# Narrow last matmuls, halved output and y steps, and a moved projection store in a GRU kernel

## The chip, the cores and the metric

The kernel runs on one core of a Trainium2 chip (trn2). The metric is the device time of one execution in microseconds; lower is better. One core has five engines that run side by side, each with its own queue in program order: PE (TensorE, matmuls), DVE (VectorE), ACT (ScalarE), POOL (GpSimd) and SP (SyncE), which here only issues DMAs. They meet through semaphores.

## The reference, cut to what matters

```python
# x: (2, 2048, 512) fp32, cond: (2, 512)
h = silu(cond @ W1.T + b1); gate = sigmoid(h @ W2.T + b2)[:, None, :]
# a Haar analysis and synthesis with every coefficient times gate: gives gate * v
x = x + (v + a)                       # v = x, so this is y = x * (2 + gate)
# GRU over 2048 time steps, batch 2, width 512, h0 = 0
vz, vr, vh = cond @ C_z + b_z, cond @ C_r + b_r, cond @ C + b
xz, xr, xh = y @ W_z, y @ W_r, y @ W  # one row for each time step
def step(h, xs):
    z = sigmoid(xz_t + h @ U_z + vz)
    r = sigmoid(xr_t + h @ U_r + vr)
    hh = tanh(xh_t + r * h @ U + vh)
    return (1.0 - z) * h + z * hh
out = y + (h of every step)
```

The steps of the GRU depend on each other, so they run one after the other: 2048 of them.

## The kernel before, in words

Width 512 lies on 128 partitions in K = 4 chunks; with batch 2 a state is 128 x 8 numbers. Each U is split into two fp16 parts, and so are h and r*h, so that sums of fp16 products have nearly fp32 accuracy. The new h is never put together for PE: it is given as four fp16 pieces (kept part high and low, new part high and low, `h_part`), r*h as two (`rh_part`).

One **step** has three products on PE, r, z and h, each of 32 matmuls of 128x128 weights (4 output chunks m, 4 input chunks k, 2 weight parts; `tile_product`, L247, the matmul is at L252). The moving operand has 8 columns (h: 4), repeated to fill WIDE = 32 columns of the output's slot in PSUM. Only the last 8 (or 4) columns of a slot and the two behind it, which ACT seeds with the input's projection (L335, L337), are read: `total` (L487) on DVE adds them up. r and h are in two halves in two banks, `staggered` (L257), so that they can start on half of their input and their first total can start early; z (L285 to L288) is one product with one total. ACT takes a tanh of each total (L351), and of z's it makes `z_keep` and `z_mul` (L368, L369), which L522 and the rest of DVE's tail need. DVE makes `rh_part` (L496, L500, L505) and at the end `h_part` (L522 to L541) and `h_cur` (L553). The first half of `h_part` releases the next step's r product. ACT also copies `h_cur` into the ring `hist` (L363).

A **block** is TB = 64 time steps: TURN = 4 steps written out (u = 0 to 3), and then GM = 12 bodies of BODY = 5 steps; NB = 32 blocks. Work beside the recurrence is put behind single steps:

- Each body makes one of the 12 tiles of the next block's input projection: in its steps u = 0 to 3 PE does one matmul (L224) of `w_stage` with `y_next` behind the h product. The tile's weights come by DMA into the one buffer `w_stage` (SP, L166), which is loaded anew for each body after the projection before it is done. In u = 0 PE waits for that load (L295) ahead of its matmul. After step u = 3 DVE stores the tile into the ring `xp` (`store_projection`, L558), after a wait for PE.
- In the turn: after step 0 PE transposes the block after next from `x_tok` into `ps_x`, and DVE makes the sum of hist and y_cur for the output, `oT` (`make_out`, L564). After step 1 PE transposes oT into `ps_o` (`put_out`), and ACT copies `y_next` to `y_cur` (L377). After step 2 ACT copies `ps_o` to `o_tok` (`put_out`, L384), and DVE makes the new `y_next` (`make_y`, L455).

**SP's queue** in a block, in this order: wait for x_tr, load the next x_tok (L131); wait for o_ev (ACT's copy to o_tok), store the output (L135, two DMAs); then twelve times: wait for proj_mm, load w_stage (L166). The queue is in order, so what is behind a wait waits too.

Of the kernel before, what the change touches and what calls it, by code (L numbers as in the profile page):

```python
# [13 lines left out]
P = 128  # L14
# [5 lines left out]
def gru_kernel(nc, x, cond, W1, b1, W2, b2, W_z, U_z, C_z, b_z, W_r, U_r, C_r, b_r, W, U, C, b, out):  # L20
# [25 lines left out]
    with ExitStack() as ctx:  # L46
# [36 lines left out]
        hist = sb("hist", [P, 2 * TB, S])  # L83
# [88 lines left out]
        @block.gpsimd  # L172
        def _(pool):
            nc.gpsimd.memset(ident[:, :], 0.0).then_inc(s["ident_zero"], 1)
            pool.wait_ge(s["ident_zero"], 1)
            nc.gpsimd.affine_select(out=ident[:, :], in_=ident[:, :], compare_op=ALU.not_equal, fill=1.0,
                                    base=0, pattern=[[-1, P]], channel_multiplier=1).then_inc(s["ident_ok"], 1)

            nc.gpsimd.memset(h_cur[:, :], 0.0)
            nc.gpsimd.memset(hist[:, TB:2 * TB, :], 0.0)  # L180
            nc.gpsimd.memset(y_cur[:, :, :], 0.0)
            nc.gpsimd.memset(h_part[:, 0:HC], 0.0).then_inc(s["hs0"], 1)
            nc.gpsimd.memset(h_part[:, HC:K], 0.0).then_inc(s["hs1"], 1)
            nc.gpsimd.memset(xp[:, :, TB:2 * TB, :], 0.0).then_inc(s["h0_ready"], 1)
            pool.wait_ge(s["umax_ok"], G)
            nc.gpsimd.partition_all_reduce(u_all[:, :], u_max[:, :], P, RMAX).then_inc(s["uall_ok"], 1)

        @block.tensor
        def _(pe):
# [40 lines left out]
            pe.wait_ge(s["y_ok"], 1)  # L230
# [16 lines left out]
            def tile_product(bank, m, g, gm, k, parts, first):  # L247

                n = (ADDENDS[g] - 1) * B
                moving = parts[:, k, :, :].rearrange("p a b -> p (a b)").unsqueeze(1).broadcast_to([P, WIDE // n, n])  # L250
                for part in range(PARTS):
                    last = nc.tensor.matmul(bank[:, SLOT * m:SLOT * m + WIDE].rearrange("p (r n) -> p r n", n=n),  # L252
                                            u_part[:, g, part, k, gm * P:(gm + 1) * P], moving,
                                            start=first and part == 0, stop=False, skip_group_check=True)
                return last

            def staggered(banks, g, parts, src, name, t1):  # L257


                def product(mh, m, kh):  # L260
                    for k in range(kh * HC, (kh + 1) * HC):
                        last = tile_product(banks[mh], m, g, mh * HC + m, k, parts, k == 0 and m == 0)
                    return last
# [15 lines left out]
            def steps(t0, count, proj=None, turn=None):  # L279
                for u in range(count):  # L280
# [4 lines left out]
                    for m in range(K):  # L285
                        for k in range(K):
                            last = tile_product(ps_z, m, Z, m, k, h_part, k == 0 and m == 0)
# [16 lines left out]
                    if turn is not None and u == 1:  # L304
                        put_out(turn[1])

            def put_out(nb):
                pe.wait_ge(s["o_sum"], nb)
# [12 lines left out]
        def _(act):  # L321
# [31 lines left out]
            def steps(t0, count, ring, turn=None):  # L353

                for u in range(count):
# [7 lines left out]
                    A(hist[:, prv, :], h_cur[:, :], ACT.Copy)  # L363
# [27 lines left out]
            A(hist[:, (T - 1) % (2 * TB), :], h_cur[:, :], ACT.Copy).then_inc(s["copied"], 1)  # L391
# [3 lines left out]
        def _(dve):  # L395
# [62 lines left out]
            make_y(1)  # L458
# [31 lines left out]
            def step(t1):  # L490
# [26 lines left out]
                total(ps_z, Z, K, "z_sum")  # L517
                dve.wait_ge(s["h0_mm"], t1)
# [36 lines left out]
            def store_projection(count, i, ring):  # L555

                dve.wait_ge(s["proj_mm"], count)
# [4 lines left out]
            def make_out(ring):  # L562

                V.scalar_tensor_tensor(oT[:, :, :], hist[:, bass.ds(ring, TB), :].rearrange("p t c -> p c t"), 1.0 / H_SCALE,  # L564
                                       y_cur[:, :, :], ALU.mult, ALU.add).then_inc(s["o_sum"], 1)

            def steps(t0, count, proj=None, turn=None):


                for u in range(count):  # L570
                    step(dve.snap(t0 + (u + 1)))
                    if proj is not None and u == K - 1:
                        store_projection(*proj)
                    if turn is not None and u == 0:

                        make_out(turn[0])
                    if turn is not None and u == 2:
                        dve.wait_ge(s["y_copied"], turn[1])
                        make_y(turn[2])

            with dve.Fori(0, NB) as n:
                other = dve.snap(((n + 1) % 2) * TB)
                steps(dve.snap(n * TB), TURN, turn=(other, dve.snap(n + 1), dve.snap(n + 2)))
                with dve.Fori(0, GM) as i:

                    steps(dve.snap(n * TB + i * BODY + TURN), BODY, proj=(dve.snap(n * GM + i + 2), i, other))
            dve.wait_ge(s["copied"], 1)
            make_out((NB - 1) % 2 * TB)
# [26 lines left out]
```

## Time and profile before

| | |
|---|---|
| median of the runs | 6800.1 us (3 runs, 6799.94 to 6800.25) |
| the profiled execution | 6811.76 us, of which the span from first to last instruction is 6809.9 |
| mean granted TensorE clock | 0.996 of full speed |
| busy | PE 5998.4 us (88%), weight loads 5642.2 (83%), DVE 4955.6 (73%), ACT 3331.6 (49%) |
| DMA | q1: 80304 packets, 129.81 MB, 5.5% of 16 engines |

How to read it: an engine's busy time is the sum over its instructions, with overlaps counted once. PE and DVE start an instruction before the one ahead has ended, so a duration is longer than the distance to the next start. On the timeline, instructions of one kind that follow each other are merged into one row: start, time from the first start to the last end, and the number behind x. The part in brackets tells how long the engine was idle before the row and what released it. The profiled execution's own time, not the median, is what the rows below add up to.

### The profile page before, as it was taken

The numbers are of one execution on the slowest core, as the hardware profiler recorded it, in microseconds if no ns is written. First come the engines' busy times: TensorE is split into PE (matmuls) and PEld (weight loads), VectorE is DVE, ScalarE is ACT, GpSimd is POOL, SyncE is SP. The second block draws the span as 40 slices with busy tenths as digits, with TensorE's granted clock in tenths as the row PEclk, the third lists the DMA queues.
The fourth block names the chain that finished last, engine by engine and source line by source line (L and its number), as shares of the span: only waits on it lengthen the run. The fifth ranks groups of instructions, "written<-read, shape, count | busy, mean of one in ns | idle before, by whom it ended". The sixth has DMA issues, their size and how long they took to land.

```text
span 6809.9 us, 488240 instructions
## 1 busy us (share of the span) xinstructions
PE 5998.4 (88%) x200232; PEld 5642.2 (83%) x200232; DVE 4955.6 (73%) x43503; ACT 3331.6 (49%) x22603; POOL 3.5 (0%) x13
## 2 busy tenths in 40 slices
PE   7888888888888888888888888888888888888888
PEld 7888888888888888888888888888888888888888
DVE  5777777777777777777777777777777777777777
ACT  3444444444444444444444444444444444444444
POOL 0000000000000000000000000000000000000000
PEclk8999999999999999999999999999999999999999
DMA  2000000000000000000000000000000000000000
GB/s 84 17 18 15 18 17 18 17 17 17 18 17 18 15 18 17 18 18 15 18 17 18 17 18 15 18 17 18 17 17 17 18 17 18 15 18 18 17 18 15
DMA packets 80315, 129.97 MB, mean 19 GB/s; under 512 B 12336, under 2 KB 18480, under 8 KB 80304
## 3 DMA queue, kind: packets, MB, share of 16 engines
q1 hardware_dynamic: 80304, 129.81, 5.5%
q8 instruction: 8, 0.13, 0.0%
q14 instruction: 3, 0.02, 0.0%
HBM read 20.46 MB, written 8.65 MB: 4 GB/s over the span
## 4 chain that ended last, share of the span: by engine, by line
PE 71%; DVE 26%; issue 3%; SPq 0%; DMA 0%; ACT 0%; ACTq 0%; DVEq 0%
PE pair_r L252 30%; PE ps_z L252 24%; PE pair_h L252 17%; DVE pair_h L487 8%; DVE h_part L522 5%; DVE h_part L541 4%; DVE h_part L527 2%; DVE keep L523 2%; DVE zn L536 2%; DVE h_part L532 2%; PE ps_z L212 0%; DMA u_raw<-in_L_cond_U 0%; PE ps_o L212 0%; DVE u_max L424 0%; PE ps_x L224 0%
## 5 line engine op out<-in xcount | busy, mean ns | idle before, releaser
L252 PEld LDWEIGHTS pair_r<-h_part,u_part 128*128 128x128 f16 x65536 | 1845.1, 96 | 1119.9 <-DVE h_part L541 1115.8
L252 PE MATMUL pair_r<-h_part,u_part 128*128 128x32 f16 x65536 | 2048.7, 177 | 771.1 <-DVE h_part L541 758.6
L252 PE MATMUL pair_h<-rh_part,u_part 128*128 128x32 f16 x65536 | 2016.6, 177 | 12.5 <-DVE rh_part L505 12.5
L252 PE MATMUL ps_z<-h_part,u_part 128*128 128x32 f16 x65536 | 1961.5, 176 | 0.0
L252 PEld LDWEIGHTS pair_h<-rh_part,u_part 128*128 128x128 f16 x65536 | 1842.8, 96 | 17.3 <-DVE rh_part L505 15.7
L252 PEld LDWEIGHTS ps_z<-h_part,u_part 128*128 128x128 f16 x65536 | 1795.3, 95 | 0.0
L487 DVE TENSOR_REDUCE pair_r<-pair_r 128x4 f32<-128x20 f32 x4096 | 759.4, 186 | 818.1 <-PE pair_r L252 615.1
L351 ACT ACTIVATE pair_r<-pair_r 128x4 f32<-128x4 f32 x4096 | 644.8, 158 | 1445.1 <-DVE pair_r L487 1182.4
L487 DVE TENSOR_REDUCE pair_h<-pair_h 128x4 f32<-128x12 f32 x4096 | 717.7, 175 | 665.7 <-PE pair_h L252 665.7
L351 ACT ACTIVATE th_z<-ps_z 128x8 f32<-128x8 f32 x2048 | 364.1, 178 | 1046.0 <-DVE ps_z L487 1046.0
L337 ACT ACTIVATE pair_h<-xp 128x8 f32 (+1 forms) x2049 | 369.9, 181 | 807.8 <-DVE zn L536 807.8
L505 DVE TENSOR_TENSOR rh_part<-rh,rh_part 128x4 f16<-128x4 f32 x4096 | 662.2, 162 | 141.1
L541 DVE TENSOR_TENSOR h_part<-zn,h_part 128x4 f16<-128x4 f32 x4096 | 669.6, 163 | 70.5
L224 PE MATMUL ps_p<-y_next,w_stage 128*128 128x128 f32 x3072 | 718.1, 316 | 0.0
L351 ACT ACTIVATE pair_h<-pair_h 128x4 f32<-128x4 f32 x4096 | 647.2, 158 | 102.2
L496 DVE SCALAR_TENSOR_TENSOR rh_part<-pair_r,h_cur 128x4 f16<-128x4 f32 x4096 | 649.6, 159 | 6.0
L532 DVE TENSOR_TENSOR h_part<-z_mul,pair_h 128x4 f16<-128x4 f32 x4096 | 625.6, 153 | 0.0
L500 DVE SCALAR_TENSOR_TENSOR rh<-pair_r,h_cur 128x4 f32<-128x4 f32 x4096 | 621.8, 152 | 0.0
L536 DVE TENSOR_TENSOR zn<-z_mul,pair_h 128x4 f32<-128x4 f32 x4096 | 619.8, 151 | 0.0
L224 PEld LDWEIGHTS ps_p<-y_next,w_stage 128*128 128x128 f32 x3072 | 458.2, 188 | 0.0
L363 ACT ACTIVATE hist<-h_cur 128x8 f32 x2048 | 428.2, 209 | 4.4
L487 DVE TENSOR_REDUCE ps_z<-ps_z 128x8 f32<-128x40 f32 x2048 | 421.8, 206 | 0.0
(70 smaller groups left out, 3275.9 us busy)
## 6 DMA issues: line engine op xcount, KB each, us to landing
w_stage<-w_in SPq DMA_DIRECT2D x384, 256.0 KB, 2.3
x_tok<-in_x SPq DMA_DIRECT2D x68, 128.0 KB, 2.6
out_dram<-o_tok SPq DMA_DIRECT2D x66, 128.0 KB, 2.3
mlp_w<-in_L_cond_W SPq DMA_DIRECT2D x2, 1024.0 KB, 6.9
u_raw<-in_L_cond_U_r SPq DMA_DIRECT2D x1, 1024.0 KB, 5.6
u_raw<-in_L_cond_U_z SPq DMA_DIRECT2D x1, 1024.0 KB, 7.6
u_raw<-in_L_cond_U SPq DMA_DIRECT2D x1, 1024.0 KB, 10.3
w_in<-in_L_cond_W_r SPq DMA_DIRECT2D x4, 256.0 KB, 9.8
```

The costliest lines, as they stand in the source:

```text
L224: return nc.tensor.matmul(bank[:, col:col + P], weight[:, k, :], y_next[:, k * B:(k + 1) * B, :].rearrange("p b t -> p (b t)"), start=(k = ...
L252: last = nc.tensor.matmul(bank[:, SLOT * m:SLOT * m + WIDE].rearrange("p (r n) -> p r n", n=n), u_part[:, g, part, k, gm * P:(gm + 1) * P] ...
L337: return A(to[:, :, :, WIDE:SLOT], src.rearrange("p (h m) b -> p h m b", h=2), ACT.Copy)
L351: A(to, bank[:, SUM:SUM + n], ACT.Tanh, scale=scale_reg[g]).then_inc(s[done], 1)
L363: A(hist[:, prv, :], h_cur[:, :], ACT.Copy)
L487: return V.tensor_reduce(bank[:, SUM:SUM + m * B].rearrange("p (m b) -> p m b", b=B), cols(bank, g, 0, m).rearrange("p m a b -> p m b a"), ...
L496: V.scalar_tensor_tensor(rh_part[:, kc[hf], 0, :], kb(ps_r[hf][:, TANH:TANH + HS]), 1.0, kb(h_cur[:, half[hf]]), ALU.add, ALU.mult)
L500: V.scalar_tensor_tensor(rh[:, half[hf]], ps_r[hf][:, TANH:TANH + HS], 1.0, h_cur[:, half[hf]], ALU.add, ALU.mult).then_inc(s[f"rh32_{hf}" ...
L505: V.tensor_tensor(rh_part[:, kc[hf], 1, :], kb(rh[:, half[hf]]), rh_part[:, kc[hf], 0, :], ALU.subtract).then_inc(s[f"rh{hf}"], 1)
L532: V.tensor_tensor(h_part[:, kc[hf], NEW, :], kb(z_mul[:, half[hf]]), kb(ps_h[hf][:, TANH:TANH + HS]), ALU.mult)
L536: V.tensor_tensor(zn[:, half[hf]], z_mul[:, half[hf]], ps_h[hf][:, TANH:TANH + HS], ALU.mult).then_inc(s[f"zn{hf}"], 1)
L541: V.tensor_tensor(h_part[:, kc[hf], NEW + 1, :], kb(zn[:, half[hf]]), h_part[:, kc[hf], NEW, :], ALU.subtract).then_inc(s[f"hs{hf}"], 1)
```

## The change

- `tile_product` takes `closing`: the last matmul (second weight part, k = 3) of the last output chunk of each total writes only the columns that are read, 8 of 32 for r and z, 4 of 32 for h. There are five in a step: r's two halves, z, h's two halves.
- `hist` has its time axis last, so that `make_out` reads it contiguously and ACT writes it with a stride.
- `make_out`, the copy to `y_cur` and `make_y` are in two halves of 4 of the 8 chunks each. make_out's are after turn steps 0 and 1, the copy's after 1 and 2, make_y's after 2 and 3. PE's `put_out` (transposes of oT) moves from after step 1 to after step 2, ACT's `put_out` (o_tok) from after step 2 to after step 3. The waits count halves.
- `store_projection` moves from the end of a body's step u = 3 into its step u = 4, right behind z's total, without the wait for proj_mm.
- SP's queue is as before.

```diff
-        hist = sb("hist", [P, 2 * TB, S])
+        hist = sb("hist", [P, S, 2 * TB])
...
-            def tile_product(bank, m, g, gm, k, parts, first):
+            def tile_product(bank, m, g, gm, k, parts, first, closing=False):
 
                 n = (ADDENDS[g] - 1) * B
-                moving = parts[:, k, :, :].rearrange("p a b -> p (a b)").unsqueeze(1).broadcast_to([P, WIDE // n, n])
+                own = parts[:, k, :, :].rearrange("p a b -> p (a b)")
+                slot = bank[:, SLOT * m:SLOT * m + WIDE]
                 for part in range(PARTS):
-                    last = nc.tensor.matmul(bank[:, SLOT * m:SLOT * m + WIDE].rearrange("p (r n) -> p r n", n=n),
-                                            u_part[:, g, part, k, gm * P:(gm + 1) * P], moving,
+                    weight = u_part[:, g, part, k, gm * P:(gm + 1) * P]
+                    if closing and part == PARTS - 1:
+
+                        return nc.tensor.matmul(slot[:, WIDE - n:WIDE], weight, own, start=False, stop=False, skip_group_check=True)
+                    last = nc.tensor.matmul(slot.rearrange("p (r n) -> p r n", n=n), weight,
+                                            own.unsqueeze(1).broadcast_to([P, WIDE // n, n]),
                                             start=first and part == 0, stop=False, skip_group_check=True)
                 return last
...
-                        last = tile_product(banks[mh], m, g, mh * HC + m, k, parts, k == 0 and m == 0)
+                        last = tile_product(banks[mh], m, g, mh * HC + m, k, parts, k == 0 and m == 0,
+                                            m == HC - 1 and k == K - 1)
...
-                            last = tile_product(ps_z, m, Z, m, k, h_part, k == 0 and m == 0)
+                            last = tile_product(ps_z, m, Z, m, k, h_part, k == 0 and m == 0, m == K - 1 and k == K - 1)
...
-                    if turn is not None and u == 1:
+                    if turn is not None and u == 2:
                         put_out(turn[1])
 
             def put_out(nb):
-                pe.wait_ge(s["o_sum"], nb)
+                pe.wait_ge(s["o_sum"], nb * 2 if isinstance(nb, int) else pe.snap(nb * 2))
...
-                y_count = pe.snap(n + 2)
+                y_count = pe.snap(n * 2 + 4)
...
-                    A(hist[:, prv, :], h_cur[:, :], ACT.Copy)
+                    A(hist[:, :, bass.ds(prv, 1)], h_cur[:, :].unsqueeze(2), ACT.Copy)
...
-                    if turn is not None and u == 1:
-                        act.wait_ge(s["o_sum"], turn)
-                        A(y_cur[:, :, :], y_next[:, :, :], ACT.Copy).then_inc(s["y_copied"], 1)
-                    if turn is not None and u == 2:
+                    if turn is not None and u in (1, 2):
+                        act.wait_ge(s["o_sum"], act.snap(turn * 2 + (u - 2)))
+                        A(y_cur[:, half[u - 1], :], y_next[:, half[u - 1], :], ACT.Copy).then_inc(s["y_copied"], 1)
+                    if turn is not None and u == 3:
                         put_out(turn)
...
-            def make_y(nb):
-
+            def make_y(part, nb, n=None):
                 dve.wait_ge(s["x_tr"], nb)
-                V.tensor_tensor(y_next[:, :, :], ps_x[:, :].rearrange("p (c t) -> p c t", t=TB),
-                                gate2[:, :].unsqueeze(2).broadcast_to([P, S, TB]), ALU.mult).then_inc(s["y_ok"], 1)
+                if n is not None:
+                    dve.wait_ge(s["y_copied"], dve.snap(n * 2 + (part + 1)))
+                V.tensor_tensor(y_next[:, half[part], :], ps_x[:, :].rearrange("p (c t) -> p c t", t=TB)[:, half[part], :],
+                                gate2[:, half[part]].unsqueeze(2).broadcast_to([P, HS, TB]), ALU.mult).then_inc(s["y_ok"], 1)
...
                 total(ps_z, Z, K, "z_sum")
+                if proj is not None:
+                    store_projection(*proj)
                 dve.wait_ge(s["h0_mm"], t1)
...
-            def store_projection(count, i, ring):
-
-                dve.wait_ge(s["proj_mm"], count)
+            def store_projection(i, ring):
+
                 V.tensor_tensor(xp[:, i, bass.ds(ring, TB), :].rearrange("p t b -> p b t"),
...
-            def make_out(ring):
-
-                V.scalar_tensor_tensor(oT[:, :, :], hist[:, bass.ds(ring, TB), :].rearrange("p t c -> p c t"), 1.0 / H_SCALE,
-                                       y_cur[:, :, :], ALU.mult, ALU.add).then_inc(s["o_sum"], 1)
+            def make_out(part, ring):
+
+                V.scalar_tensor_tensor(oT[:, half[part], :], hist[:, half[part], bass.ds(ring, TB)], 1.0 / H_SCALE,
+                                       y_cur[:, half[part], :], ALU.mult, ALU.add).then_inc(s["o_sum"], 1)
...
-                    step(dve.snap(t0 + (u + 1)))
-                    if proj is not None and u == K - 1:
-                        store_projection(*proj)
-                    if turn is not None and u == 0:
-
-                        make_out(turn[0])
-                    if turn is not None and u == 2:
-                        dve.wait_ge(s["y_copied"], turn[1])
-                        make_y(turn[2])
+                    step(dve.snap(t0 + (u + 1)), proj if u == K else None)
+                    if turn is not None and u < 2:
+                        make_out(u, turn[0])
+                    if turn is not None and u >= 2:
+                        make_y(u - 2, turn[2], turn[1])
```

## Rows read from the trace of the kernel before

**Rows 1.** Page, the chain that ended last: share of the span by engine.
```profile
PE 71%; DVE 26%; issue 3%; SPq 0%; DMA 0%; ACT 0%; ACTq 0%; DVEq 0%
```

**Rows 2.** Timeline, a plain step: start us, us, engine, line, op, out<-in, count [idle<-releaser].
```profile
3011.66 1.00 PE L252 MATMUL pair_r<-h_part,u_part 128*128 128x32 f16 x32 [0.31 <-DVE h_part L541]
...
3012.39 0.49 DVE L487 TENSOR_REDUCE pair_r<-pair_r 128x4 f32<-128x20 f32 x2 [0.38 <-PE pair_r L252]
...
3012.51 0.96 PE L252 MATMUL ps_z<-h_part,u_part 128*128 128x32 f16 x32
...
3013.41 0.16 DVE L505 TENSOR_TENSOR rh_part<-rh,rh_part 128x4 f16<-128x4 f32 x1
3013.50 0.21 DVE L487 TENSOR_REDUCE ps_z<-ps_z 128x8 f32<-128x40 f32 x1
3013.75 0.18 ACT L351 ACTIVATE th_z<-ps_z 128x8 f32<-128x8 f32 x1 [0.52 <-DVE ps_z L487]
...
3014.03 0.18 DVE L487 TENSOR_REDUCE pair_h<-pair_h 128x4 f32<-128x12 f32 x1 [0.32 <-PE pair_h L252]
...
3014.12 0.30 PEld L224 LDWEIGHTS ps_p<-y_next,w_stage 128*128 128x128 f32 x2
...
3014.20 0.17 DVE L522 TENSOR_TENSOR h_part<-z_keep,h_cur 128x8 f16<-128x8 f32 x1
...
3014.92 1.00 PE L252 MATMUL pair_r<-h_part,u_part 128*128 128x32 f16 x32 [0.30 <-DVE h_part L541]
```

**Rows 3.** Timeline, the next step, which has the projection's store; last row: next r.
```profile
3015.51 0.29 DVE L558 TENSOR_TENSOR xp<-ps_p,v_bias 128x128 f32 x1 [0.24 <-issue]
3015.72 0.42 DVE L487 TENSOR_REDUCE pair_r<-pair_r 128x4 f32<-128x20 f32 x2
...
3017.04 0.18 ACT L351 ACTIVATE th_z<-ps_z 128x8 f32<-128x8 f32 x1 [0.55 <-DVE ps_z L487]
...
3017.54 0.17 DVE L522 TENSOR_TENSOR h_part<-z_keep,h_cur 128x8 f16<-128x8 f32 x1
...
3018.26 0.52 PE L252 MATMUL pair_r<-h_part,u_part 128*128 128x32 f16 x13 [0.64 <-DVE h_part L541]
```

**Rows 4.** Timeline, turn step 1, with make_out; first and last row: its r and the next.
```profile
3021.54 1.00 PE L252 MATMUL pair_r<-h_part,u_part 128*128 128x32 f16 x32
...
3021.85 1.09 DVE L564 SCALAR_TENSOR_TENSOR oT<-hist,y_cur 128x512 f32<-128x512 f32 x1
...
3025.36 0.29 PE L252 MATMUL pair_r<-h_part,u_part 128*128 128x32 f16 x5
```

**Rows 5.** Timeline, turn step 3: r, make_y, o_tok, SP's queue, and the next r.
```profile
3028.62 1.00 PE L252 MATMUL pair_r<-h_part,u_part 128*128 128x32 f16 x32 [0.62 <-DVE h_part L541]
...
3028.89 0.68 DVE L455 TENSOR_TENSOR y_next<-ps_x,gate 128x512 f32<-128x512 f32 x1
3028.94 0.59 ACT L384 ACTIVATE o_tok<-ps_o 128x512 f32<-128x512 f32 x1
...
3029.75 1.27 SPq L135 DMA_DIRECT2D out_dram<-o_tok  x2
...
3031.39 0.53 SPq L166 DMA_DIRECT2D w_stage<-w_in  x1
...
3032.00 0.27 PE L252 MATMUL pair_r<-h_part,u_part 128*128 128x32 f16 x4 [0.62 <-DVE h_part L541]
```

**Rows 6.** Line 558, 3015.0 to 3015.9: ns min/median/max, first to last start, of register code.
```profile
L558 DVEq FUSED_REGOPS  x2: 52/112/173, 3015.2 to 3015.4; - x2
```

**Rows 7.** DMA issues from 3025 to 3040: count, KB each, median us to landing.
```profile
w_stage<-w_in SPq DMA_DIRECT2D x1, 256.0 KB, 2.3
```

**Rows 8.** Timeline of PE, the first step of all and the start of the second.
```profile
74.90 1.03 PE L252 MATMUL pair_r<-h_part,u_part 128*128 128x32 f16 x32 [3.88 <-issue]
...
78.36 0.81 PE L252 MATMUL pair_r<-h_part,u_part 128*128 128x32 f16 x23
```

**Rows 9.** Windows: us, busy of PE, PEld, DVE, ACT, POOL, granted clock, DMA share, GB/s.
```profile
75.00:79.00 4.00, 4.00 (x123) 3.91 (x123) 2.79 (x22) 1.65 (x11) 0.00 (x0) 0.51 0.01 4
```

More of the change, by code:

```diff
@@ L179, in _ @@
             nc.gpsimd.memset(h_cur[:, :], 0.0)
-            nc.gpsimd.memset(hist[:, TB:2 * TB, :], 0.0)
+            nc.gpsimd.memset(hist[:, :, TB:2 * TB], 0.0)
             nc.gpsimd.memset(y_cur[:, :, :], 0.0)
@@ L229, in _ @@
             pe.wait_ge(s["w_ok"], G)
-            pe.wait_ge(s["y_ok"], 1)
+            pe.wait_ge(s["y_ok"], 2)
             pe.wait_ge(s["gate_ok"], 1)
@@ L390, in _ @@
             act.wait_ge(s["h_ok"], T)
-            A(hist[:, (T - 1) % (2 * TB), :], h_cur[:, :], ACT.Copy).then_inc(s["copied"], 1)
+            A(hist[:, :, (T - 1) % (2 * TB)], h_cur[:, :], ACT.Copy).then_inc(s["copied"], 1)
             put_out(NB + 1)
@@ L450, in _ @@
             dve.wait_ge(s["gate_ok"], 1)
-            def make_y(nb):
+            def make_y(part, nb, n=None):
                 dve.wait_ge(s["x_tr"], nb)
-                V.tensor_tensor(y_next[:, :, :], ps_x[:, :].rearrange("p (c t) -> p c t", t=TB),
-                                gate2[:, :].unsqueeze(2).broadcast_to([P, S, TB]), ALU.mult).then_inc(s["y_ok"], 1)
-            make_y(1)
+                if n is not None:
+                    dve.wait_ge(s["y_copied"], dve.snap(n * 2 + (part + 1)))
+                V.tensor_tensor(y_next[:, half[part], :], ps_x[:, :].rearrange("p (c t) -> p c t", t=TB)[:, half[part], :],
+                                gate2[:, half[part]].unsqueeze(2).broadcast_to([P, HS, TB]), ALU.mult).then_inc(s["y_ok"], 1)
+            for part in range(2):
+                make_y(part, 1)
             for g in range(G):
@@ L488, in total, with step @@
                                        cols(bank, g, 0, m).rearrange("p m a b -> p m b a"), AX_X, ALU.add).then_inc(s[done], 1)
-            def step(t1):
+            def step(t1, proj):
                 kc = (slice(0, HC), slice(HC, K))
@@ L560, in store_projection @@
                                 v_bias[:, i, :].unsqueeze(2).broadcast_to([P, B, TB]), ALU.add)
-            def make_out(ring):
-                V.scalar_tensor_tensor(oT[:, :, :], hist[:, bass.ds(ring, TB), :].rearrange("p t c -> p c t"), 1.0 / H_SCALE,
-                                       y_cur[:, :, :], ALU.mult, ALU.add).then_inc(s["o_sum"], 1)
+            def make_out(part, ring):
+                V.scalar_tensor_tensor(oT[:, half[part], :], hist[:, half[part], bass.ds(ring, TB)], 1.0 / H_SCALE,
+                                       y_cur[:, half[part], :], ALU.mult, ALU.add).then_inc(s["o_sum"], 1)
             def steps(t0, count, proj=None, turn=None):
                 for u in range(count):
-                    step(dve.snap(t0 + (u + 1)))
-                    if proj is not None and u == K - 1:
-                        store_projection(*proj)
-                    if turn is not None and u == 0:
-                        make_out(turn[0])
-                    if turn is not None and u == 2:
-                        dve.wait_ge(s["y_copied"], turn[1])
-                        make_y(turn[2])
+                    step(dve.snap(t0 + (u + 1)), proj if u == K else None)
[3 more added lines that the diff above has]
+                        make_y(u - 2, turn[2], turn[1])
             with dve.Fori(0, NB) as n:
                 other = dve.snap(((n + 1) % 2) * TB)
-                steps(dve.snap(n * TB), TURN, turn=(other, dve.snap(n + 1), dve.snap(n + 2)))
+                steps(dve.snap(n * TB), TURN, turn=(other, n, dve.snap(n + 2)))
                 with dve.Fori(0, GM) as i:
-                    steps(dve.snap(n * TB + i * BODY + TURN), BODY, proj=(dve.snap(n * GM + i + 2), i, other))
+                    steps(dve.snap(n * TB + i * BODY + TURN), BODY, proj=(i, other))
             dve.wait_ge(s["copied"], 1)
-            make_out((NB - 1) % 2 * TB)
+            for part in range(2):
+                make_out(part, (NB - 1) % 2 * TB)
 _INS = ["x", "cond_1024", "L0_cond_W1", "L0_cond_b1", "L0_cond_W2", "L0_cond_b2",
```

## The prediction, made before the changed kernel was run

> **What bounds the kernel now.** I read the chain of waits first: PE holds 71% of the chain that ended last and DVE 26%, DMA nothing [rows 1]. So one recurrent step, 2048 times in a row, sets the time. Then I read a plain step on the timeline [rows 2]. From one start of the r product (3011.66) to the next (3014.92) it takes 3.26 us. PE streams r, z and h, then totals on DVE, tanhs on ACT and the tail on DVE release the next r. The wait that ends last in it is z's: z's product ends at 3012.51+0.96 = 3013.47, its total starts at 3013.50, th_z at 3013.75, and L522, which needs ACT's z_keep, at 3014.20, 0.72 us ahead of the next r. DVE is free for z's total at about the same time, since L505 starts at 3013.41 and a DVE instruction can start 0.08 us before the one ahead of it ends (L558 ends at 3015.80, the total behind it starts at 3015.72 [rows 3]).
>
> Third, I compare steps by their r starts. The step with the projection's store takes 3018.26-3014.92 = 3.34 [rows 2, 3]. The four turn steps take 3.28, 3.82, 3.26 and 3.38 [rows 3 to 5]. The others are plain: one block is 4 turn steps and 12 bodies of 5 steps, 32 times. Last, I read SP's queue: nearly idle, but it feeds w_stage [rows 5].
>
> **Narrow closing matmul, L252.** Five products a step get a last matmul of 8 (h: 4) columns instead of 32. PE's stream is not shortened by it: r's 32 matmuls start within 3012.51-3011.66 = 0.85 us, at most 27 ns each [rows 2], and no row shows them closer. Only the end of each product can come earlier. The bounds: nothing, and 24/32 of 27 ns, 20 ns. I take 10 ns, the middle, which is also one column per cycle at the full clock of 2.4 GHz. Then r's totals, L505 and z's total come 10 ns earlier and take th_z, z_keep and L522 along. 2048 x 0.010 = 20.5 us gained, between 0 and 41.
>
> The Trainium skill (TensorE: Matmul & The Clock Gate, "Single matmul latency") gives a latency of (398+N)/2.4 ns; by it 24 columns are 10 ns. No row here has a narrower fp16 matmul to compare.
>
> **Output and y in halves, L564, L455.** L564 starts at 3021.85, 0.31 into turn step 1, and takes 1.09; total r0 should start 3012.39-3011.66 = 0.73 in [rows 2, 4]. The step is longer by 0.56. y's 0.68 us make step 3 longer by 0.12 [rows 5]. A half has 256 elements. From 128 elements in 0.29 (L558) and 512 in 0.68 (L455), 256 take 0.42; at L564's strided pace they take 0.16+0.93/2 = 0.62. A half that starts at 0.31 frees DVE at 0.65 or at 0.85, against 0.73. The new hist layout makes the reads contiguous, so I take the first: hidden in all four steps, (0.56+0.12) x 32 = 21.8 us gained. By the other end two halves would cost 0.12 each, 8 us. ACT's halves of y_cur and its strided write of hist fall where ACT waits for totals. The new waits are met beforehand: ahead of each half of y DVE waits for a copy that ACT made one step earlier, and PE's transposes of oT, now after step 2, wait for halves made after steps 0 and 1. The 0.02 of turn step 0 has none of this in it and stays.
>
> The Trainium skill (SBUF — State Buffer, "Door 1: The DMA port swizzle") says that each access that crosses to a new 16-byte line pays a penalty. hist was read 32 bytes apart; 1.09 us against 0.68 for as many elements agrees, and by the rule the halves are at the fast end.
>
> **Projection's store behind z's total, L558.** The store step is 0.08 longer, but part of it isn't the store: from th_z to L522 it takes 3017.54-3017.04 = 0.50 against 0.45 in the plain step [rows 2, 3], all of it ACT's own work, so that stays. The store's share is that th_z comes 2.12 into the step instead of 2.09, 0.03 to 0.04 with the rounding. 384 x 0.035 = 13.4 us gained if the new place hides it. There DVE is free from z's total (1.83 into the step after the change) to h0's total (now 3014.03, 2.37 in; then some 2.35). The store's address code starts at 3015.2 and is two pieces, 52 and 173 ns, the store at 3015.51: 0.30 with gaps [rows 3, 6]. The store holds DVE for 0.29-0.08 = 0.21. 1.83+0.02+0.30+0.21 = 2.36: it just fits, and L522 behind it waits for ACT until 2.6.
>
> **The step that is moved with them: o_tok on ACT, and SP behind it.** put_out on ACT moves from after turn step 2 to after turn step 3. SP's queue is left as it is, and in order: wait for o_tok, store the output (L135, two DMAs), and only then load w_stage for body 0 (L166). Before, o_tok starts at 3028.94, the stores go from 3029.75, L166 at 3031.39 [rows 5], and its data land 2.3 later [rows 7], at 3033.7. A projection comes 3014.12-3011.66 = 2.46 into its step [rows 2], here 3032.00+2.46 = 3034.46: 0.8 us to spare. After the change the same row of events hangs on the r start of body step 0 as it hung on 3028.62: the data land 3031.39+2.3-3028.62 = 5.07 into that step, and the projection wants them at 2.46. PE waits, and behind it in its queue stands the next step's r product, for which DVE and ACT wait in turn. PE goes on at 5.07+0.03, the projection's weight loads take 0.30 [rows 2], so r starts at 5.40 instead of 3.25: 2.15 us lost per block, x 32 = 68.8 us.
>
> PE then stands idle for some 2.4 us in each block. Recurrent steps at half clock are seen only at the start: after 3.88 us of idle PE the clock is at 0.51, and the step from 74.90 to 78.36 takes 3.46 instead of turn step 0's 3.28 [rows 8, 9]. I count one such step per block, 0.17 x 32 = 5.5 us, with bounds of none and two.
>
> **Sum.** The profiled execution took 6811.8 us (span 6809.9), 11.7 above the median of the runs; the terms are counts of steps, so I put them against the median. 6800.1 - 20.5 - 21.8 - 13.4 + 68.8 + 5.5 = 6818.7, say 6818, with 6806 to 6830 for the clock's bounds and some ns in each term. About 0.2%, 13.6 us, is what a measurement of this kernel can tell from no change, so this is just slower.
>
> **Rivals.**
> - *No earlier ends.* What ends a product is the way through PE and the semaphore, not the columns. For it: r's last matmul ends 3011.66+1.00-3012.51 = 0.15 after z's first has started [rows 2], so most of a matmul's time isn't its columns. Then 20.5 us are missing: 6839. Chance 0.17.
> - *Store collides with h0's total.* The address code is longer in the new place. For it: the fit above has no spare. If it takes half as long again, 0.15, of which ACT's lateness hides 0.04, 384 x 0.11 = 42 us come on top: 6860. Chance 0.08.
> - *No stall, so faster.* The one mechanism is SP's: if w_stage has landed 2.46 into body step 0, the 68.8 and the 5.5 fall away: 6744. It needs L166 issued by 2.46-2.3 = 0.16 into that step, while o_tok starts only 0.32 into it. Each 0.1 us beyond costs 3.2 us, so faster by 0.2% needs a stall under 1.3 us. Rows 5 show nothing that lets SP pass the store. Chance 0.08.
> - *Terms a little better*: the clock stays up, the columns are worth up to 20 ns, or the stall is 0.2 us shorter: 6795 to 6812, no difference that can be measured. Chance 0.15.
>
> **How the numbers follow.** The forecast has 0.52; a third of its 6806 to 6830 lies within 0.2%. Slower: 0.35+0.17+0.08 = 0.60. Same: 0.17+0.13 = 0.30. Faster: 0.08+0.02 = 0.10. The range, 6795 to 6842, takes in the bounds of the columns and of the clock; it leaves out the faster case and the full collision.
>
> **What would show it.** Right: once a block PE idle for some 2.4 us ahead of L224, ended by the DMA of w_stage; plain steps of 3.25, turn steps of 3.27 and three of 3.25, a store step of 3.29 to 3.30; z's total 1.83 into a step; h0's total in the store step not behind 2.37; halves of 0.42. A mean granted clock under the 0.996 of before would show the clock's term. Wrong: plain steps still of 3.26 (columns), a store step above 3.34 (collision), no DMA among the releasers of L224 (no stall), many steps at half clock, each 0.17 us.

## The result and the profile after

| | before | after |
|---|---|---|
| median of the runs | 6800.5 us (6 runs) | 6839.7 us (6835.6 to 6845.6, 6 runs) |
| ratio to before | | 1.0058, 95% interval 1.0045 to 1.0071 |
| the profiled execution | 6811.8 us, span 6809.9 | 6840.6 us, span 6838.8 |
| mean granted TensorE clock | 0.996 | 0.957 |

The kernel became slower by 39.2 us, 0.58%. The kernel before runs some 10 us longer at some times than at others (medians of 6799.8 and of 6809.6 on the same chip), and its trace is of a long run, which is why the two spans lie only 28.9 us apart. Ratios below are to runs of before made together with the kernel named. The line numbers of the kernel after: matmuls L257, the narrow one L256, totals L495, tanhs L357, L522 is now L532, the store L558 is L567, make_out L573, make_y L462, o_tok L390.

The waits of the kernel after over its whole execution (engine, line, what it waited for: us in total, times, longest) show one wait that was not there before:

```profile
PE pair_r L257 <- DVE h_part L551: 723.7, 1840, 0.7
...
PE ps_p L224 <- DMA w_stage<-w_in: 83.7, 32, 3.8
```

PE waits 32 times, once a block, 2.6 us each, for the load of w_stage. The timeline of one body step 0 (rows of PE, ACT and SP; it answers to rows 5, which showed turn step 3 before):

```profile
3043.47 0.67 PE L257 MATMUL pair_r<-h_part,u_part 128*128 128x32 f16 x19 [0.63 <-DVE h_part L551]
3043.79 0.59 ACT L390 ACTIVATE o_tok<-ps_o 128x512 f32<-128x512 f32 x1
...
3044.60 1.27 SPq L135 DMA_DIRECT2D out_dram<-o_tok  x2
...
3045.92 0.16 PE L256 MATMUL pair_h<-rh_part,u_part 128*128 128x4 f16 x1
3046.24 0.53 SPq L166 DMA_DIRECT2D w_stage<-w_in  x1
3048.67 0.50 PEld L224 LDWEIGHTS ps_p<-y_next,w_stage 128*128 128x128 f32 x2 [2.67 <-issue]
3048.67 0.79 PE L224 MATMUL ps_p<-y_next,w_stage 128*128 128x128 f32 x2 [2.59 <-DMA w_stage<-w_in]
3049.05 0.82 PEld L257 LDWEIGHTS pair_r<-h_part,u_part 128*128 128x128 f16 x19
3049.26 0.71 PE L257 MATMUL pair_r<-h_part,u_part 128*128 128x32 f16 x19
```

It reads as forecast: o_tok 0.32 into the step, the stores at 1.13, L166 at 2.77, its data 2.31 later at 5.08, and the projection, wanted at 2.46, starts at 5.20. The next r starts 5.79 after this one, 0.59 behind the projection.

Here the granted clock went to half at 3048.63, just ahead of the projection. In the block shown next it did so only behind r's start (1782.28 on this timeline), and r comes 0.32 behind the projection, 5.53 into the step:

```profile
1776.31 0.68 PE L257 MATMUL pair_r<-h_part,u_part 128*128 128x32 f16 x19 [0.63 <-DVE h_part L551]
...
1781.52 0.48 PE L224 MATMUL ps_p<-y_next,w_stage 128*128 128x128 f32 x2 [2.60 <-DMA w_stage<-w_in]
1781.84 0.65 PE L257 MATMUL pair_r<-h_part,u_part 128*128 128x32 f16 x19
```

A plain step after, on the timeline (it answers to rows 2), and below it the halves and the store by line:

```profile
3072.22 0.67 PE L257 MATMUL pair_r<-h_part,u_part 128*128 128x32 f16 x19 [0.31 <-DVE h_part L551]
...
3073.86 0.17 PE L256 MATMUL ps_z<-h_part,u_part 128*128 128x8 f16 x1
...
3074.06 0.21 DVE L495 TENSOR_REDUCE ps_z<-ps_z 128x8 f32<-128x40 f32 x1
3074.30 0.18 ACT L357 ACTIVATE th_z<-ps_z 128x8 f32<-128x8 f32 x1 [0.51 <-DVE ps_z L495]
...
3075.47 0.67 PE L257 MATMUL pair_r<-h_part,u_part 128*128 128x32 f16 x19 [0.30 <-DVE h_part L551]
```

```profile
L256 PE MATMUL pair_r<-h_part,u_part 128*128 128x8 f16 x4096 | 680.5, 166 | 0.0
...
L567 DVE TENSOR_TENSOR xp<-ps_p,v_bias 128x128 f32 x384 | 112.1, 292 | 47.0
...
L573 DVE SCALAR_TENSOR_TENSOR oT<-hist,y_cur 128x256 f32<-128x256 f32 x66 | 27.7, 422 | 0.4 <-ACT hist L397 0.4
L462 DVE TENSOR_TENSOR y_next<-ps_x,gate 128x256 f32<-128x256 f32 x66 | 27.7, 420 | 0.2 <-PE ps_x L194 0.2
```

The step takes 3.25 us, the halves 0.42 each, as forecast, and the narrow matmul lasts 166 ns.

All traces together, from one r product's first matmul to the next one's (ns; turn and body steps are means over blocks 2 to 32, the plain and the store step medians, so that single falls of the clock don't enter there). The last column has the number and the sum of the stretches at half clock, 1.2 of 2.4 GHz, after the first 100 us; each such stretch is called a fall below. The last of them reaches to the end of the execution, when the steps are over; before has no other.

| kernel | turn steps 0, 1, 2, 3 | body 0, step 0 | step 1 | plain | store | half clock |
|---|---|---|---|---|---|---|
| before | 3285, 3825, 3258, 3382 | 3258 | 3258 | 3259 | 3340 | 1, 9 us |
| after | 3341, 3264, 3244, 3244 | 5757 | 3347 | 3245 | 3289 | 132, 543 us |
| o_tok back | 3324, 3265, 3244, 3394 | 3279 | 3263 | 3243 | 3288 | 108, 373 us |
| o_tok late only | 3282, 3825, 3256, 3378 | 5652 | 3334 | 3254 | 3331 | 32, 139 us |
| closing only | 3405, 3720, 3250, 3372 | 3317 | 3296 | 3245 | 3331 | 277, 997 us |
| after, no closing | 3274, 3255, 3253, 3254 | 5774 | 3368 | 3255 | 3299 | 32, 195 us |
| closing, 40 columns | 3277, 3821, 3247, 3371 | 3246 | 3250 | 3246 | 3338 | 1, 6 us |
| z only, 40 columns | 3284, 3831, 3266, 3386 | 3264 | 3267 | 3267 | 3333 | 1, 7 us |
| all but z, 40 columns | 3273, 3818, 3263, 3370 | 3259 | 3262 | 3262 | 3338 | 1, 8 us |
| store only | 3285, 3831, 3258, 3383 | 3257 | 3257 | 3257 | 3304 | 1, 6 us |
| halves, load first | 3275, 3256, 3258, 3259 | 3258 | 3257 | 3258 | 3341 | 1, 8 us |
| 24 columns | 3483, 3743, 3282, 3403 | 3353 | 3351 | 3352 | 3392 | 31, 6501 us |
| after, 40 columns | 3261, 3250, 3246, 3246 | 5679 | 3756 | 3246 | 3292 | 31, 156 us |
| after, load first, 40 columns | 3261, 3247, 3249, 3250 | 3249 | 3248 | 3250 | 3292 | 1, 7 us |

### The profile page after: what moved, and what is told of

Its sections match the earlier page's. It is cut to its first block, busy times and chain, and to the rows that moved or that the text cites. A ratio compares the mean times of both kernels' runs of the same rounds, so it can differ in the third digit from the quotient of the medians.

```text
span 6838.8 us, 488018 instructions
## 1 busy us (share of the span) xinstructions
PE 5991.9 (88%) x200232; PEld 5641.6 (82%) x200232; DVE 4947.4 (72%) x43569; ACT 3310.3 (48%) x22635; POOL 3.5 (0%) x13
## 4 chain that ended last, share of the span: by engine, by line
PE 64%; DVE 28%; issue 3%; ACT 3%; DMA 1%; SPq 1%; ACTq 0%; DVEq 0%
PE pair_r L257 28%; PE ps_z L257 19%; PE pair_h L257 13%; DVE pair_h L495 6%; DVE h_part L532 5%; DVE h_part L551 4%; DVE h_part L537 2%; DVE keep L533 2%; DVE rh_part L513 2%; DVE zn L546 2%; DVE h_part L542 2%; PE ps_p L224 1%; DMA w_stage<-w_in 1%; DVE pair_r L495 1%; ACT pair_r L343 1%
## 5 line engine op out<-in xcount | busy, mean ns | idle before, releaser
L257 PEld LDWEIGHTS pair_r<-h_part,u_part 128*128 128x128 f16 x61440 | 1805.0, 96 | 1080.1 <-DVE h_part L551 1072.6
L257 PE MATMUL pair_r<-h_part,u_part 128*128 128x32 f16 x61440 | 2004.7, 178 | 735.0 <-DVE h_part L551 723.7
L257 PE MATMUL pair_h<-rh_part,u_part 128*128 128x32 f16 x61440 | 1936.5, 177 | 0.0
L257 PE MATMUL ps_z<-h_part,u_part 128*128 128x32 f16 x63488 | 1918.2, 177 | 0.0
L257 PEld LDWEIGHTS pair_h<-rh_part,u_part 128*128 128x128 f16 x61440 | 1771.3, 96 | 0.0
L257 PEld LDWEIGHTS ps_z<-h_part,u_part 128*128 128x128 f16 x63488 | 1751.9, 96 | 0.0
L495 DVE TENSOR_REDUCE pair_r<-pair_r 128x4 f32<-128x20 f32 x4096 | 765.5, 187 | 1044.9 <-PE pair_r L256 804.7
L357 ACT ACTIVATE pair_r<-pair_r 128x4 f32<-128x4 f32 x4096 | 647.2, 158 | 1497.1 <-DVE pair_r L495 1224.1
L495 DVE TENSOR_REDUCE pair_h<-pair_h 128x4 f32<-128x12 f32 x4096 | 713.1, 174 | 514.3 <-PE pair_h L256 514.3
L357 ACT ACTIVATE th_z<-ps_z 128x8 f32<-128x8 f32 x2048 | 364.0, 178 | 1029.9 <-DVE ps_z L495 1029.9
L224 PE MATMUL ps_p<-y_next,w_stage 128*128 128x128 f32 x3072 | 760.7, 331 | 83.7 <-DMA w_stage<-w_in 83.7
L357 ACT ACTIVATE pair_h<-pair_h 128x4 f32<-128x4 f32 x4096 | 647.1, 158 | 128.8
L256 PE MATMUL pair_r<-h_part,u_part 128*128 128x8 f16 x4096 | 680.5, 166 | 0.0
L256 PE MATMUL pair_h<-rh_part,u_part 128*128 128x4 f16 x4096 | 672.3, 164 | 0.0
L542 DVE TENSOR_TENSOR h_part<-z_mul,pair_h 128x4 f16<-128x4 f32 x4096 | 621.8, 152 | 0.1
L224 PEld LDWEIGHTS ps_p<-y_next,w_stage 128*128 128x128 f32 x3072 | 486.7, 200 | 86.3 <-issue 86.3
## 6 DMA issues: line engine op xcount, KB each, us to landing
u_raw<-in_L_cond_U SPq DMA_DIRECT2D x1, 1024.0 KB, 11.1
```

The costliest lines, as they stand in the source:

```text
L224: return nc.tensor.matmul(bank[:, col:col + P], weight[:, k, :], y_next[:, k * B:(k + 1) * B, :].rearrange("p b t -> p (b t)"), start=(k = ...
L256: return nc.tensor.matmul(slot[:, WIDE - n:WIDE], weight, own, start=False, stop=False, skip_group_check=True)
L257: last = nc.tensor.matmul(slot.rearrange("p (r n) -> p r n", n=n), weight, own.unsqueeze(1).broadcast_to([P, WIDE // n, n]), start=first a ...
L357: A(to, bank[:, SUM:SUM + n], ACT.Tanh, scale=scale_reg[g]).then_inc(s[done], 1)
L495: return V.tensor_reduce(bank[:, SUM:SUM + m * B].rearrange("p (m b) -> p m b", b=B), cols(bank, g, 0, m).rearrange("p m a b -> p m b a"), ...
L542: V.tensor_tensor(h_part[:, kc[hf], NEW, :], kb(z_mul[:, half[hf]]), kb(ps_h[hf][:, TANH:TANH + HS]), ALU.mult)
```

## The experiments

The theory was this: the loss is the stall behind o_tok; the three edits proper each gain what the steps show; and a second loss is in the clock, since the trace of after falls to half clock 132 times where before it fell once, at its end. The stall explains at most one fall a block, so either the narrow matmuls cause the rest, or the falls have one cause and follow the stall in ways not seen. The first four kernels tell these apart.

**o_tok back.** The kernel after, with ACT's copy where it was:

```diff
-                    if turn is not None and u == 3:
+                    if turn is not None and u == 2:
                         put_out(turn)
```

> The changed kernel with one thing undone: ACT copies o_tok after turn step 2 again. Theory (the load of w_stage stands behind o_tok and the output's store in SP's queue): the stalled step of 5.9 us a block goes back to 3.25, 2.65 us x 32 = 85 us less than the changed kernel, about 6754; PE waits for no DMA ahead of L224; some falls of the clock stay, because the narrow closing matmuls stream fewer columns: mean clock about 0.98. Rival (the falls of the clock come only from PE's idle time in the stall): mean clock 0.996 again, as before the change, and 6744. Rival (the stall has another cause, such as the wait for y in halves): about 6840 still.

Measured: 6760.0 us, ratio 0.9942 (0.9926 to 0.9959), mean clock 0.970; no wait for w_stage is left. That is 79.7 less than after, against 85 expected. The difference is a new cost in turn step 3, 3394 ns instead of 3244, 4.8 us over 32 blocks. Its timeline, r to r:

```profile
3002.63 0.67 PE L257 MATMUL pair_r<-h_part,u_part 128*128 128x32 f16 x19
3002.95 0.40 ACT L383 ACTIVATE y_cur<-y_next 128x256 f32<-128x256 f32 x1
...
3003.25 0.58 ACT L390 ACTIVATE o_tok<-ps_o 128x512 f32<-128x512 f32 x1
3003.35 0.49 DVE L495 TENSOR_REDUCE pair_r<-pair_r 128x4 f32<-128x20 f32 x2
3003.73 0.30 ACT L357 ACTIVATE pair_r<-pair_r 128x4 f32<-128x4 f32 x2
...
3006.02 0.24 PE L257 MATMUL pair_r<-h_part,u_part 128*128 128x32 f16 x3 [0.62 <-DVE h_part L551]
```

The half of y_cur and o_tok now stand behind the same step on ACT, and r's tanh starts 0.38 after its total instead of 0.22 (3013.33 to 3013.55 in a plain step of the same trace). So the copy's new place had its use. The rival by which the falls come only from the stall is out: without a stall 107 remain, and the one at the end.

**o_tok late only.** The kernel before, with that one edit:

```diff
-                    if turn is not None and u == 2:
+                    if turn is not None and u == 3:
                         put_out(turn)
```

> The kernel before with this alone: ACT copies o_tok after turn step 3 instead of step 2. Theory: r of body step 1 starts 5.55 us after that of step 0 instead of 3.26, and the half clock after it costs 0.3 us more: 2.6 us x 32 = +84, about 6884. If the stall needs the halves or the moved transposes: 6800.

Measured: 6880.5 us, ratio 1.0119 (1.0102 to 1.0136), +80.7 us, near the 84 expected, with one fall at each stall. One moved line of ACT costs it all; halves, transposes and store are not needed for it. The waits of this kernel:

```profile
PE ps_p L224 <- DMA w_stage<-w_in: 82.7, 32, 3.2
```

**Closing only.** The kernel before with the changed `tile_product` and the two places that use it. Cut to the line that matters:

```diff
+                    if closing and part == PARTS - 1:
+
+                        return nc.tensor.matmul(slot[:, WIDE - n:WIDE], weight, own, start=False, stop=False, skip_group_check=True)
```

> The kernel before with the narrow closing matmuls alone. Theory: plain steps 3.244 instead of 3.258 us, 2048 x 0.014 = -29; the clock falls for one stretch some two or three times a block, +10: about 6782, clock about 0.98. Rival (falls come from the stall only): no fall after the first 100 us, 6772. Rival (columns bring nothing): 6800 and steps of 3.258.

Measured: 6810.9 us, ratio 1.0015 (1.0006 to 1.0025), +11.1 where -18 was expected. The plain step is as expected, 3245 against the 3255 of the kernels with full matmuls that ran together with it (o_tok late only; after, no closing): 10 ns. But the clock fell 277 times, not two or three times a block, and stood at half for 997 us. Windows of the granted clock around one of these stretches (us, busy of PE, PEld, DVE, ACT, POOL, granted clock, DMA share, GB/s):

```profile
3029.00:3032.40 3.40, 2.78 (x104) 2.65 (x101) 2.44 (x24) 1.63 (x12) 0.00 (x0) 1.00 0.56 154
3032.50:3035.90 3.40, 3.40 (x107) 3.14 (x104) 2.43 (x23) 1.63 (x12) 0.00 (x0) 0.50 0.00 0
3035.90:3039.30 3.40, 3.08 (x111) 2.89 (x108) 2.46 (x22) 1.56 (x11) 0.00 (x0) 1.00 0.00 0
```

With 10 ns x 2048 = 20 us gained and 11 lost on the whole, the falls cost 31 us, 0.11 us each. They come in 235 of the 384 bodies, and 224 of the 277 start in a body's step 0, behind the store step, the one step with no projection's matmul behind h. I had read the number of falls to expect off the kernel after, where that step is 3289 ns long; here the store is in its old place and it is 3331. Whether that difference is why there are more falls here, no run shows.

**After without closing.** All calls pass `closing` as False.

```diff
-                                            m == HC - 1 and k == K - 1)
+                                            False)
...
-                            last = tile_product(ps_z, m, Z, m, k, h_part, k == 0 and m == 0, m == K - 1 and k == K - 1)
+                            last = tile_product(ps_z, m, Z, m, k, h_part, k == 0 and m == 0, False)
```

> The changed kernel with full closing matmuls. Theory: plain steps 3.258, and the clock falls only once a block, behind the stall: 6840 + 29 - 10 = about 6858, clock about 0.975. Rival (falls have nothing to do with the columns): as many falls as in the changed kernel, about four a block, and 6869.

Measured: 6855.6 us, ratio 1.0079 (1.0062 to 1.0096), clock 0.982, and no fall but those at the stalls and the end. The narrow matmuls are what adds the 100 other falls. Taking them out costs 15.9 us over after, where 18 were expected (the intervals of the two ratios overlap a little): in the change as a whole they seem to gain more than their falls cost.

The second four ask whether it is the number of columns, and which of the five closing matmuls matter.

**Closing, 40 columns.** The closing-only kernel with one constant changed. The extra columns are copies that nothing reads, as the ones before.

```diff
-    WIDE = 32
+    WIDE = 40
```

> The kernel before with the narrow closing matmuls, and all other matmuls of the step 40 columns wide instead of 32. Theory (the clock falls because PE streams too few columns in a stretch): no fall after the first 100 us, plain steps stay 3.244, 6800 - 29 = 6771. Rival (it is the narrow matmul itself that upsets the clock, or the shorter step): about as many falls as with 32 columns, 277 of them, and 6811. Rival (40 columns no longer fit the pace of 25 ns): each step longer by up to 96 x 3 ns, over 7000.

Measured: 6791.3 us, ratio 0.9975 (0.9965 to 0.9984), -18.2 us; no fall between the start and the end, clock 0.996, plain step 3246. The narrow matmul is harmless once the others carry more columns, and 40 still fit the pace. The gain is smaller than the 29 I had written. That took 3258 and 3244 from the two first traces, which are not of runs made together; and not every step gains as much. A plain step gains 12 ns (3246 against 3257 or 3258 in before, store only and halves), but the store step only 2 (3338 against 3340), and the mean block of the trace is 209.63 us long against 210.23 before: 19 us in 32 blocks.

**Only z narrow**, and **all but z narrow**, both with 40 columns:

> As b2 but narrow only in z's last matmul. Theory (z's total is the last wait of the step and the h0 chain 11 ns behind it): plain steps 3.247, about 11 of the 14 ns, 6800 - 23 = 6777. Rival (r's and h's chain is the last): 3.258, 6800.

> As b2 but narrow in r's and h's last matmuls and not in z's. Theory: nothing gained, z's last matmul with 40 columns ends 3 ns later than with 32: plain steps 3.258 to 3.262, 6800 to 6808. Rival (r's and h's chain is the last): 3.247, 6777.

Measured: z only 6821.6 us, ratio 1.0019 (1.0010 to 1.0029), 12 us slower than before; all but z 6812.2, ratio 1.0005 (0.9995 to 1.0014). Neither alone gains anything, and z only, of which I expected most of the gain, loses. Two chains meet at L538 (the first product of z_mul with tanh of h0): z's, through z_keep, L528 (its product with h_cur, L522 in the kernel before) and DVE's own sequence, and h0's, through its total and tanh. The timeline with z only:

```profile
3059.53 0.16 ACT L357 ACTIVATE pair_h<-pair_h 128x4 f32<-128x4 f32 x1
3059.62 0.17 DVE L493 TENSOR_REDUCE pair_h<-pair_h 128x4 f32<-128x12 f32 x1
3059.71 0.16 DVE L538 TENSOR_TENSOR h_part<-z_mul,pair_h 128x4 f16<-128x4 f32 x1
3059.79 0.15 DVE L542 TENSOR_TENSOR zn<-z_mul,pair_h 128x4 f32<-128x4 f32 x1
```

and with all five narrow (closing, 40 columns):

```profile
3059.52 0.16 ACT L357 ACTIVATE pair_h<-pair_h 128x4 f32<-128x4 f32 x1
3059.65 0.17 DVE L493 TENSOR_REDUCE pair_h<-pair_h 128x4 f32<-128x12 f32 x1
3059.73 0.15 DVE L538 TENSOR_TENSOR h_part<-z_mul,pair_h 128x4 f16<-128x4 f32 x1
3059.80 0.15 DVE L542 TENSOR_TENSOR zn<-z_mul,pair_h 128x4 f32<-128x4 f32 x1
```

In the second L538 follows the total on DVE's own queue (0.08), and h0's tanh has ended 0.05 before. In the first DVE is through sooner, but h0's tanh ends at 3059.69, and L538 starts 0.02 behind it: h0's chain is the last. The medians of 1356 plain steps of each trace say the same (ns from the start of r; L538 is L532 in the kernel before):

| kernel | z's total starts | h0's tanh ends | L538 starts | from there to the next r |
|---|---|---|---|---|
| before | 1844 | 2742 | 2786 | 472 |
| z only | 1836 | 2754 | 2786 | 481 |
| all but z | 1848 | 2722 | 2789 | 473 |
| all five | 1834 | 2723 | 2774 | 472 |

With z only, L538 waits for the tanh, starts 32 ns behind its end and so no earlier than before. What stands behind it comes 9 ns later, since a DVE instruction that starts out of a wait is followed later by the next one (76 ns from L538 to L542 instead of 66). That is the step of 3267 instead of 3258. In the kernel before the tanh ended 44 ns ahead of L532, 12 more than those 32: the two chains were that close, and only both together move the step. Why h0's tanh ends 12 ns later with z only than before is settled in part: 40-column matmuls last 3 ns longer than those of 32 (179 ns against 176 in the traces), in r's product and in h's.

**After, load first, 40 columns.** The change as a whole, with both losses mended:

```diff
+                sp.wait_ge(s["proj_mm"], sp.snap(n * GM + 1))
+                sp.dma_start(w_stage[:, :, :], w_in[:, 0]).then_inc(s["wst_in"], 16)
                 sp.wait_ge(s["o_ev"], sp.snap(n + 1))
                 store_out(sp.snap((n + (NB - 1)) % NB))
-                with sp.Fori(0, GM) as i:
+                with sp.Fori(1, GM) as i:
...
-    WIDE = 32
+    WIDE = 40
```

> The changed kernel with SP loading w_stage for body 0 ahead of the wait for o_tok and the output's store, and 40 columns instead of 32. Theory: neither the stall (2.65 us a block) nor the falls are left, all that the edits save in steps remains: block of 208.2 us instead of 210.2, 6800 - 65 = 6735. Rival (the load has other reasons to be late, or is slowed by the x_tok load beside it): over 6800.

Measured: 6751.6 us, ratio 0.9915 (0.9899 to 0.9932), 58.0 less than before beside it and the shortest time of all. PE waits for no load of w_stage, the clock is 0.996, and a block takes 208.4 us instead of 210.2. It beats both kernels. That is 7 us less than the 65 expected: its plain steps take 3250 and not the 3244 that I had put in.

The last four price the two other edits alone, and try the clock from the other side.

**Store only.** The kernel before with the store moved. Cut to the lines that place it:

```diff
+                if proj is not None:
+                    store_projection(*proj)
                 dve.wait_ge(s["h0_mm"], t1)
```

> The kernel before with the projection's store behind z's total, alone. Theory: the store step goes from 3.34 to 3.30 us, 384 x 0.038 = 15 us less: a ratio to the kernel before of 0.998; h0's total in the store step about 2.38 us in, hidden. Rival (the store collides with h0's total): the store step 3.34 or more, ratio 1.000 or above.

Measured: 6794.1 us, ratio 0.9980 (0.9970 to 0.9989), -14.7 us; store step 3304. As expected, with no collision.

**Halves, load first.** The halves with all that belongs to them (the layout of hist, the moved copies and transposes), and SP's load as in the diff of the load-first kernel.

> The kernel before with the halves of output and y alone, o_tok after turn step 3 as in the changed kernel, but SP loads w_stage for body 0 ahead of the output's store. Theory: turn steps 1 and 3 go from 3.83 and 3.38 to 3.26: 0.69 us x 32 = 22 us less, ratio 0.9968, no stall in body step 0. Rival (halves don't fit beside the step): turn steps 1 and 2 above 3.3 each, ratio 0.998 or more.

Measured: 6785.8 us, ratio 0.9965 (0.9953 to 0.9978), -22.9 us; turn steps 3256, 3258 and 3259. As expected.

**24 columns.** The kernel before with WIDE = 24 and nothing else.

> The kernel before with all matmuls of the step 24 columns wide instead of 32 (the columns left out are copies that nothing reads); no narrow closing matmul. Theory (too few columns in a stretch bring the clock down): the clock falls in nearly every body and often, mean clock under 0.9, and although every product's end comes 3 ns earlier the kernel is slower by 50 us or more. Rival (falls come from the narrow matmul itself): no falls after the first 100 us, plain steps 3 to 4 ns shorter, 7 us less.

Measured: 6979.0 us, ratio 1.0249 (1.0232 to 1.0266), clock 0.516. The page's line of the clock, in 40 slices, and a window of a block:

```profile
PEclk6555555555555555555555555555555555555555
```

```profile
3110.00:3300.00 190.00, 182.96 (x5533) 169.49 (x5533) 136.90 (x1200) 90.66 (x620) 0.00 (x0) 0.50 0.04 15
```

There is no narrow closing matmul in it, so the number of columns is enough to bring the clock down. It did not fall again and again, as I wrote, but fell once a block, in turn step 2 or 3, and stayed down until the next turn. A plain step at half clock takes 3.35 us, 0.09 more.

**After, 40 columns.** The stall stays, the columns are mended.

> The changed kernel with 40 columns instead of 32. Theory: only the falls behind the stall are left, about 32 of them, one a block; the stalled pair of steps stays 2.6 us too long: 6840 less about 14, ratio to the kernel before about 1.003 to 1.004. Rival (the falls in the bodies cost nothing): ratio 1.0058 as for the changed kernel.

Measured: 6852.1 us, ratio 1.0062 (1.0045 to 1.0079); 0.3 to 0.4% was expected. The other falls in the bodies are gone; one is left behind each stall but one, and the one at the end. But there 40 columns cost more: body steps 0, 1 and 2 take 5679, 3756 and 3453 ns on average instead of 5757, 3347 and 3285 in after, 0.50 us a block, 16 us, which is more than was gained. A step that is wholly at half clock takes 3950 ns instead of 3350. PE's rows behind one stall, with the r product still at full clock and the h product at half (the clock fell at 3055.30):

```profile
3053.30 0.48 PE L224 MATMUL ps_p<-y_next,w_stage 128*128 128x128 f32 x2 [2.59 <-DMA w_stage<-w_in]
3053.62 0.63 PE L257 MATMUL pair_r<-h_part,u_part 128*128 128x40 f16 x19
...
3055.23 0.78 PE L257 MATMUL pair_h<-rh_part,u_part 128*128 128x40 f16 x19
```

At full clock 19 matmuls span 0.63 us, at half clock 0.78. Less 0.18 for the last one alone, that is 25 and 33 ns from start to start, and 40 columns at 1.2 GHz are 33 ns: they fit the pace at full clock and no longer at half.

## Why the prediction was right, and where it was off

The forecast was 6818, slower, in a range of 6795 to 6842; measured 6839.7, slower by 39.2 where 18 were forecast. The sign, the cause and most terms held; the clock's term was too small behind the stall and missing in the bodies, and the stall's was a little too small. That 6839.7 still lies within the range is partly luck: the range's upper end was made for columns that bring nothing, not for a clock that falls in the bodies.

- **Stall.** Right in every part of its chain: L166 2.77 into body step 0, the data there at 5.08, the projection held in PE's queue with the next r behind it, alone worth +80.7 us. Mis-sized: I let r start at 5.40. The projection starts 0.12 behind its data, not 0.03, and r 0.32 behind it where the clock is still full: 5.53, which is 2.28 late, 73 us instead of 68.8.
- **Clock behind the stall.** Forecast as one slow step a block, 0.17 (rows 8 give 0.18), 5.5 us. A step at half clock costs less, 0.10 (3347 against 3245). But in 26 of 31 stalls the clock is down before the projection starts, and then its weight loads take 0.50 instead of 0.30 and r starts 0.58 behind it instead of 0.32: 0.23 on average. Together 0.33 a block, 11 us.
- **Clock in the bodies.** Missing. The step of the prediction that failed is the one on the closing matmul: it asked what fewer columns do to a product's end and not what they do to the clock, though rows 9 had shown half clock at work. Some 100 further falls come from it (after against after, no closing); with 0.11 us each, as in the closing-only run, that is 11 us. Many steps at half clock was among the prediction's own signs of being wrong, and it is the one that came.
- **Closing matmul.** 10 ns a step, taken as the middle of 0 to 20: measured 10 between kernels run together, z's total starting 1834 ns into a step instead of 1844, which is 20 us against 20.5; with 40 columns, alone, 18. The middle of a range was a guess that came out. The reason given was half the truth. z's chain was last, but h0's was 12 ns behind it, which the prediction never looked at; had the diff narrowed z alone, next to nothing would have been gained.
- **Halves** 21.8 forecast, 22.9 measured alone. **Store** 13.4 forecast, 14.7 alone; in the kernel after h0's total in the store step came at 2.37, 0.02 later than in a plain step and still hidden behind z_keep, as allowed for. The 0.04 that I left with ACT stayed (3289 against 3245).
- **Rivals.** *No earlier ends* is out by z's total, which starts 10 ns earlier, and the shorter step, though its time, 6839, is by chance the one measured. *Collision* and *no stall* are out by store only and by the waits.

The sum with the measured terms: -20 (closing) -22.9 (halves) -14.7 (store) +73 (stall) +11 (clock behind it) +11 (clock in the bodies) = +37, against +39.2 with an interval of +31 to +48.

The Trainium skill's latency of (398+N)/2.4 ns (TensorE: Matmul & The Clock Gate, "Single matmul latency") gives 10 ns for 24 columns, and the 10 ns of z's total agree; so do the narrow matmul's 166 against 177 ns, though the ends of matmuls are modelled in a profile.

The Trainium skill's advice against falls of the clock (TensorE: Matmul & The Clock Gate, "Why this matters for your kernels") is to leave no long idle gap in PE. Here PE was idle for 2.6 us where the falls at the stall came, but ahead of those in the bodies its gaps were no longer than before (0.63 us), and what had changed was the number of columns.

## What to carry to other kernels

When a step is put later in one engine's queue, follow what other queues do in order behind it: a load with nothing to do with it can stand there, and the distance to its deadline is the number to compute. Columns that nothing reads may be what keeps TensorE's clock up: here 24 instead of 32 took its mean from 0.996 to 0.516. So before taking them out look at the granted clock and price a fall. And before taking a few ns off the last wait, look for the chain right behind it; here neither of the two gained alone, and both together 12 ns in a plain step.

## What was not expected of the hardware

- The clock fell to half with no longer gap in PE than before. Narrowing 5 of 96 matmuls a step from 32 to 8 or 4 columns gave 277 falls (997 us at half clock), and 24 columns in all of them half clock nearly throughout (0.516). With 40 columns in the other 91 of 96 there was none.
- Half clock costs little in a stream of 32-column matmuls (3350 ns for a step wholly at half clock against 3245), and much more with 40 columns (3950 against 3246).
- In 26 of 31 stalls the clock was down before PE had its first matmul after 2.6 us of idle time, so that restart itself was slow (0.58 us from the projection to r instead of 0.32).
- 40 columns leave the 25 ns pace of the 32-column matmuls at full clock as it is, but each matmul lasts 3 ns longer (179 against 176).
